# GNN layer on one Trainium2 core: side work of VectorE and GpSimd ahead of the edge loop spread between node pairs

## The reference

```python
h = jnp.maximum(_layernorm(x, axis=-1), 0.0)
eq = h @ Wq + bq
ek = h @ Wk + bk
e = efeat @ We + be
m = jax.nn.relu(eq[dst] + ek[src] + e)
ft = jax.ops.segment_sum(m, dst, num_segments=n_nodes)
x = x + (ft @ Wr + br)
```

## Time and profile before

| | us |
|---|---|
| median of 3 runs | 1139.0 |
| lowest and highest run | 1137.21, 1139.22 |
| profiled execution, device time | 1140.08 |
| its span, first to last instruction | 1138.2 |
| TensorE, busy share of the span | 96% |
| GpSimd, busy share | 75% |
| VectorE, busy share | 82% |
| ScalarE, busy share | 77% |

### The profile page before, as it was taken

The page is one execution under the profiler, slowest core; times in us unless marked ns, Lnnn a source line. Parts: engine busy times, 40 slices in busy tenths (PEclk is TensorE's granted clock), DMA queues, the critical chain, the costliest instruction groups (busy, mean ns, idle before and its releaser), DMA issues.

```text
span 1138.2 us, 28524 instructions
## 1 busy us (share of the span) xinstructions
PE 1095.3 (96%) x9096; PEld 1078.0 (95%) x9096; DVE 938.7 (82%) x1362; ACT 880.0 (77%) x1560; POOL 848.9 (75%) x946
## 2 busy tenths in 40 slices
PE   7869999999999999999999999999999999999998
PEld 7859999999999999999999999999999999998997
DVE  6677888888888888888888888888888888878877
ACT  5766787787788878778878777878778788777774
POOL 7767777777777777777777777777777777777773
PEclk8899999999999999999999999999999999999999
DMA  8679999899889999898899999989998898987882
GB/s 263 196 249 279 285 288 279 276 287 283 280 280 283 286 279 286 278 283 285 280 282 280 287 273 284 287 275 289 281 281 281 274 286 277 285 278 249 276 248 88
DMA packets 171234, 309.22 MB, mean 272 GB/s; under 512 B 30801, under 2 KB 117470, under 8 KB 171150
## 3 DMA queue, kind: packets, MB, share of 16 engines
q1 hardware_dynamic: 130990, 199.18, 52.8%
q0 software_dynamic: 39888, 108.97, 34.2%
q10 hardware_dynamic: 272, 0.26, 0.1%
HBM read 281.20 MB, written 27.08 MB: 271 GB/s over the span
## 4 chain that ended last, share of the span: by engine, by line
POOL 37%; DVE 21%; issue 20%; DMA 15%; PE 5%; ACT 1%; POOLq 0%; DVEq 0%; ACTq 0%
POOL k_rows L676 36%; DVE p_edge L1091 18%; DMA k_rows<-k_table,idx 14%; PE p_sum L1243 2%; PE p_edge L1243 1%; DVE hT_lo L1122 1%; PE p_turn L1263 1%; PE p_sum L1335 0%; DMA ft<-in_x 0%; POOL hn L621 0%; DVE m_lo L1100 0%; DVE stats L932 0%; POOLq L299 0%; DVE edge_lo L1069 0%; DMA k_table<-k_rows 0%
## 5 line engine op out<-in xcount | busy, mean ns | idle before, releaser
L676 POOL DMA_INDIRECT k_rows<-k_table,idx x815 | 777.3, 954 | 248.4 <-issue 183.2
L1243 PE MATMUL p_edge<-we_hi,edge_hi 128*128 128x256 f32 x1662 | 476.7, 287 | 24.7 <-DVE m_lo L1100 14.5
L1243 PE MATMUL p_edge<-we_lo,edge_hi 128*128 128x256 f32 x1662 | 465.1, 280 | 0.0
L1243 PE MATMUL p_edge<-we_hi,edge_lo 128*128 128x256 f32 x1662 | 464.5, 279 | 0.0
L1091 DVE TENSOR_TENSOR p_edge<-p_edge,k_rows 128x1024 f32<-128x1024 f32 x208 | 256.0, 1231 | 164.7 <-DMA k_rows<-k_table,idx 140.3
L1243 PEld LDWEIGHTS p_edge<-we_hi,edge_hi 128*128 128x128 f32 x1662 | 314.5, 189 | 38.4 <-issue 26.6
L806 ACT ACTIVATE m_hi<-p_edge 128x1024 fp32r<-128x1024 f32 x208 | 213.5, 1026 | 165.9 <-DVE p_edge L1091 165.9
L1243 PEld LDWEIGHTS p_edge<-we_lo,edge_hi 128*128 128x128 f32 x1662 | 315.2, 190 | 0.0
L1243 PEld LDWEIGHTS p_edge<-we_hi,edge_lo 128*128 128x128 f32 x1662 | 313.3, 189 | 0.0
L1069 DVE TENSOR_TENSOR edge_lo<-edge,edge_hi 128x1024 fp32r<-128x1024 f32 x208 | 253.2, 1218 | 1.9 <-ACT edge_hi L755 1.8
L1100 DVE SCALAR_TENSOR_TENSOR m_lo<-p_edge,m_hi 128x1024 fp32r<-128x1024 f32 x208 | 252.7, 1215 | 0.4 <-ACT m_hi L806 0.4
(11 more groups left out here) (138 smaller groups left out, 1108.3 us busy)
## 6 DMA issues: line engine op xcount, KB each, us to landing
edge<-in_edges SPq DMA_DIRECT2D x208, 512.0 KB
rel_row<-rel_table SPq DMA_DIRECT2D x208, 96.0 KB
q_win<-q_table SPq DMA_DIRECT2D x416, 48.0 KB
k_rows<-k_table,idx POOLq DMA_INDIRECT x815
q_table<-hn SPq DMA_DIRECT2D x46, 256.0 KB
pre<-in_x SPq DMA_DIRECT2D x55, 128.0 KB, 3.8
out_rows<-pre SPq DMA_DIRECT2D x55, 128.0 KB, 1.7
k_table<-k_rows SPq DMA_DIRECT2D x25, 256.0 KB, 3.2
```

The lines of the kernel that those rows point to most:

```text
L676: nc.gpsimd.indirect_dma_start(out=k_rows[:, slot, j, :], out_offset=None, in_=k_table, in_offset=bass.IndirectOffsetOnAxis(ap=offsets, ax ...
L1243: ins = nc.tensor.matmul(target, a(h), b[:, h, :], start=(start and h == 0 and n == 0), stop=(stop and h == HALVES - 1 and n == 2))
```

## The change

Everything it touches lies ahead of the loop; the loop's own lists are the same. On **GpSimd** the even block of pair 4 goes to ScalarE (`POOL_FROM` = 5) and those of pairs 14 to 19 go to VectorE (`VECTOR_PAIRS`, new function `vector_centre`); variance of part 2 comes after the centre of pair 5, the constants move to step 17, one clear each to steps 15 and 17, and the other five come after the last centre. On **VectorE** reductions are cut in halves, the window work starts one step later, and the operations that took a scalar or were a cast (`window_starts`, `group_nodes`, `window_table`) become ones with two tensor inputs. The roots come at other steps and the reciprocals have steps of their own. **SyncE** issues the fifth part of x at the start, the ranges two steps and one step later, one edge load each at steps 10 and 19, and two after the `rel_row` loads. **TensorE** turns 40 identities instead of 24 and 8 more before pair 0. The block without nodes (block 49, of pair 24 in step 22) gets no k product, copy or store, and in the last step the second block's product goes to a PSUM bank of its own, so that the first can be copied and stored while it runs.

```diff
-POOL_FROM = 4
+SLOT_CLEARS = 2
+POOL_FROM = 5
-ROOT_STEPS = (None, 1, 4, 6, 10, 13)
+VECTOR_PAIRS = range(14, 20)
+ROOT_STEPS = (None, 1, 3, 7, 13, 16)
+INVERSE_STEPS = (None, 1, 4, 8, 14, 17)
-WARM_TURNS = 24
+WARM_TURNS = 40
+WARM_BETWEEN = 8
+EMPTY_BLOCK = -(-NODES // LANES)
+EMPTY_STEP = PAIR_ORDER.index(EMPTY_BLOCK // 2)
...
+        def k_place(i, j):
+            if i == NODE_PAIRS - 1 and j == 1:
+                return p_turn[:, 1, 0:D]
+            return p_sum[:, i % 2, j * D:(j + 1) * D]
...
-                if i == 12:
-                    sp.wait_ge(s_prep, 2)
+                if i == 8:
+                    sp.dma_start(src_idx[:], src_lanes).then_inc(s_lanes, 16)
+                if i == 10:
+                    load_edge(0, 0)
+                if i == 14:
+                    sp.wait_ge(s_prep, 2 * CHUNKS)
                     sp.dma_start(range_table[0].rearrange("(p c) -> p c", c=CHUNKS), low_g[:]).then_inc(s_range, 16)
                     sp.dma_start(range_table[1].rearrange("(p c) -> p c", c=CHUNKS), top_g[:]).then_inc(s_range, 16)
-                if i == 14:
+                if i == 15:
                     sp.wait_ge(s_range, 32)
...
-                if i in (15, 16, 17, 18):
-                    load_edge(0, i - 15)
+                if i == 17:
+                    sp.dma_start(dst_idx[:], dst_lanes).then_inc(s_lanes, 16)
+                if i == 19:
+                    load_edge(0, 1)
...
             for u in range(UNROLL):
                 load_row(0, u)
+            for u in range(2, UNROLL):
+                load_edge(0, u)
...
+            def vector_centre(i):
...
+                nc.vector.scalar_tensor_tensor(hn[:, k % NRING, :], x_all[:, BLOCK_ORDER[k], :], at(minus_mean, k),
+                                               nought[:].to_broadcast([LANES, D]), ALU.add, ALU.max).then_inc(s_hn0, 1)
...
-                nc.vector.tensor_scalar(win_f[:], ranges[:, 0, :], float(NODES - WIN), narrow[:],
-                                        ALU.min, ALU.mult).then_inc(s_prep, 1)
+                for starts in (win_f, win_tab):
+                    nc.vector.scalar_tensor_tensor(starts[:], ranges[:, 0, :], float(NODES - WIN),
+                                                   narrow[:].to_broadcast([LANES, GROUPS]),
+                                                   ALU.min, ALU.mult).then_inc(s_prep, 1)
...
             for i in range(NODE_PAIRS):
                 h_lo(i)
+                if i + 2 in VECTOR_PAIRS:
+                    vector_centre(i + 2)
...
-                if i == 18:
+                if i == 19:
                     widest_span()
...
-                for j in range(2):
+                for j in range(1 if i == EMPTY_STEP else 2):
...
+            turn_ident(WARM_TURNS)
             turn_h(0)
             turn_h(1)
+            turn_ident(WARM_BETWEEN)
```

168 lines of the change are left out of this document (99 added, 69 removed).

## The result

| | before | after |
|---|---|---|
| median of the runs | 1138.71 us (11 runs, 1135.91 to 1139.47) | 1134.67 us (11 runs, 1132.59 to 1136.3) |
| profiled execution, device time | 1140.08 us | 1135.05 us |
| its span | 1138.2 us | 1132.9 us |
| first gather | 76.95 us | 69.41 us |
| first gather to the end | 1061.2 us | 1063.5 us |

The ratio is 0.9966, with a 95% interval of 0.9955 to 0.9976. The kernel is faster by some 4 us (5.3 us between the two profiled spans), where 11 were forecast. The forecast of 1128.0 us, with a range of 1124.8 to 1133.0, was too low, and the time lies outside the range.

A forecast was written before the change was run, and what follows sets the result against it. GpSimd's gathers set the pace, so the gain is an earlier first gather: 11.1 us at pair 24 plus 0.4, less 0.5 in the loop, gives 11.0. From the median of 1139.0 that makes 1128.0 us, range 1124.8 to 1133.

The forecast's parts named there:

- the early clock: TensorE ahead of pair 0: more identities keep 2.4 GHz, so pair 0 starts at 11.2 us, not 11.70; failure rival 0.08.
- Pairs 0 to 19: Ahead of the loop: pair 0 at 11.2 us, pair 4 at 20.3, pair 12 at 36.5, pair 19 at 49.6.
- pair 4's new wait: ScalarE's root at step 3 waits for GpSimd's variance of part 2: pair 4 at 20.3 us instead of 19.2, 1.1 lost.
- the centres on VectorE: Even centres from pair 14 on, made by VectorE: 0.3 to 0.6 us each, 0.4 taken; pair 19 at 49.6 us.
- The ranges: Ahead of pair 20: landing 2.1 us, load 4.3; VectorE waits 1.7, pair 20 starts at 52.9 us, not 51.5, 1.4 lost.
- Full clock to the end: TensorE ahead of the loop: clock expected at full from 16 to 60 us, neither stretch of 1.2 GHz returning.
- a rival with 0.15 and 1132.2 us: Ahead of pair 20: ranges take 4.8 us to land, TensorE's pause brings half clock costing 1.5 us; chance 0.15.
- The last stores: End of pair 24: last k store follows 2.2 us after the pair's start instead of 2.56, a gain of 0.4 us.
- TensorE's start and the loop: Loop start: two edge loads ahead of the q stores make TensorE slip 1 to 2 us against the gathers, costing 0.5 us.
- this rival: Loop start: q stores slip over 5.1 us, the fifth gather waits and each further us is lost; 1134 with 11, chance 0.05.
- The rival with that mechanism: Loop's first 200 us: late TensorE stretches gathers; at 0.97 us mean over 831 it costs 16 us, time 1144; chance 0.04.
- The forms: VectorE's window operations with two tensor inputs: about 0.4 us each instead of 1.35, no longer delaying pairs 21 to 24.

The follow-up runs named there:

- two close variants: Kernel before with edge loads 2 and 3 moved behind the rel_row loads, ratio 0.9987; kernel before with only the two-tensor window operations, ratio 1.0003.

## Why the prediction was right and wrong

The steps that failed lie behind pair 19. The landing and load of the ranges were put too short, the half clock that followed the longer pause was taken as not coming, the last two stores were priced too low, and TensorE's later start was priced at 0.5 us in the loop, which became 2.3 us longer as gathers were stretched.

**What bounds the kernel: right.** The first gather and the pace of the gathers set the end; the last gather is as far from it as before.

**Pairs 0 to 19: right within 0.5 us,** with the early clock held (of three stretches of half clock before, the prediction saw two), pair 4's new wait (1.27 us for the variance), and the centres on VectorE at 0.48 instead of 0.4. Undone one at a time, the identities were worth 1.0 us of the first gather and the centres 2.6. The loss of 1.1 us that was put on pair 4's wait was real at pair 4 and worth nothing later: without it the same time is lost at pair 7, where a copy waits for a k store. The prediction had named such a copy as what would make it wrong; in after one waits too, for 0.56 us ahead of pair 7, and it did little harm.

**The ranges: the mechanism right, the terms too small.** It was forecast that VectorE would wait with the low part of pair 20 behind it. The landing was put at 2.1 us and was 3.0 (3.2 to 4.6 in the kernels of the other sets), the load at 4.3 and was 5.0, and the second store was issued 0.5 later: 2.0 us. The end of 4.8 us that the prediction kept for the landing was nearer to most of what the sets showed than the value taken.

**Full clock to the end: wrong.** The pause ahead of pair 20 brought 1.2 GHz back, which is most of the 1.6 us from pair 20 to pair 24. The prediction had this as a rival with 0.15 and 1132.2 us, tied to a landing of 4.8 us; it came with 3.0. It had the row for it, 2.5 us of pause ahead of pair 7; the pause became 2.8 us, and the 2 us by which the ranges were late made it so. Where the window work came one step later neither the long pause nor the half clock came, so the two failures were one.

**The last stores: 0.9 us too few.** Two stores in place of one were counted as half a product won. The first of them held SyncE for 1.47 us, and the second stood behind it for 1.1 us. In the other traces of the changed kernel the first took 1.5 to 1.6, with the window work later 0.33, as the second did; what holds it is open.

**TensorE's start and the loop: wrong in size.** A slip of 1 to 2 us was forecast for edge loads 2 and 3 ahead of the q stores, and it was 4.3: the first q store was issued 1.4 us behind the first gather instead of 0.1 ahead of it, and from there to the first window load it took 6.9 us (70.83 to 77.73) instead of 4.2. In both kernels TensorE also began the loop at half clock, up to 90.7 us before and 87.0 after. The prediction looked at the fifth group's room of 5.1 us as the point from which it costs; 0.95 us of that were left and no gather waited for an `add_rows`, so this rival did not come, by little. What it took as a side effect of 0.5 us was the cost: gathers stretched by `edge_lo` as long as TensorE is behind, 2.7 us more in the first 64. The rival with that mechanism was priced for all 831 gathers and for slower; it came, for the first 60 or so.

Together: 0.4 + 1.6 + 1.6 + 0.9 - 0.5 ahead of the loop and 1.8 in it are 5.8, which is, to rounding, the 11.0 forecast less the 5.3 between the spans. The medians are only 4.0 apart, as the profiled execution of the kernel before was 1.4 us above its median and that of after 0.4. So part of the miss may lie in the start of the sum: it took the first gather of one trace, 76.95, where two close variants had 75.75 and 74.81.

**The forms: right in size, underrated.** The operations were put at 0.4 us each instead of 1.35, and `win_f` took 0.36. In their new place they carried the change: without them the first gather, with the clears in a row, came 6.0 us later.

The fastest of the kernels run, by its median, is the changed one with the window work one step later, the variance first and the edge loads at SyncE's steps 18 and 20: 1130.79 us, 0.9926 [0.991, 0.9942] of the kernel before.

## What to carry to other kernels

When work is moved on two engines at once, price each operation by what runs beside it in its new place: an operation of VectorE that took 1.4 us beside one clear took 6.05 us beside five. A transfer that others wait for belongs ahead of the bulk loads of its queue, and its landing is to be taken from rows behind an equally busy queue, not from the fastest. And a stage that starts late costs not only where someone waits for it: until it has caught up, its neighbours run in another phase, so look at what they then collide with.

## What the runs showed of the hardware that was not expected

- A VectorE operation with a scalar (104x512) that started with five clears of GpSimd in a row took 6.05 us and ended 0.28 us after the last; the next one took 0.47 with GpSimd idle. With two tensors both took 1.28 together beside the same clears. With GpSimd idle the scalar form on 128x208 is the faster, 0.32 against 0.36.
- Gathers that start inside `edge_lo`, with two SBUF inputs, took up to 2.01 us instead of 0.95 in the usual loop; of 6256 that started inside `add_rows` or `m_lo`, with one PSUM input, none took over 0.96.
- Stores of 832 bytes had landed after 3.0 to 4.6 us in the changed kernel and its variants, and after 5.4 to 7.5 where three edge loads of 512 KB stood ahead of them.
- A pause of TensorE of 1.4 us left the clock at 2.4 GHz; pauses of 2.8 and 3.25 us were followed by 1.2 GHz. In between it went either way: of the pauses ahead of the first gather, one of 1.98 us and seven of 2.19 to 2.57 were followed by it, and those of 1.99, 2.02, 2.11 and 2.61 were not. Turned identities alone brought the full clock, 4.7 to 7.4 us after the start.
- The loop of every kernel was 270 us longer in four of five sets, once on a chip that had the usual loop in another. TensorE then stood still within bodies, and 87 to 114 us of it were stretched gathers; the cause is open.
